# A recommendation model's count matmuls, split into two halves of the partitions

## The chip, the cores and the metric

The kernel runs on one core of a Trainium2 chip. The metric is device time in microseconds (us) from the start to the end of the program. The engines are called PE (TensorE, matmuls), DVE (VectorE), ACT (ScalarE), POOL (GpSimd) and SP (SyncE, which only issues DMAs here). They run side by side and wait for each other through semaphores.

## The reference

A model of the kind used for recommendations. There are 2048 samples, 26 tables of 12500 rows of 64 numbers, and for each sample and table 20 indices, whose rows are summed ("pooled").

```python
x = _mlp(dense_x, bot, sigmoid_last=False)                  # 13 -> 512 -> 256 -> 64
pooled = jax.vmap(lambda tab, ix: jnp.take(tab, ix, axis=0).sum(axis=1))(tables, indices)
Tcat = jnp.concatenate([x[:, None, :], jnp.transpose(pooled, (1, 0, 2))], axis=1)
Z = jnp.einsum('bim,bjm->bij', Tcat, Tcat)
li, lj = jnp.tril_indices(ni, k=-1)
R = jnp.concatenate([x, Z[:, li, lj]], axis=1)
return _mlp(R, top, sigmoid_last=True)                      # 415 -> 512 -> 256 -> 1
```

## The kernel before, in words

Of the 26 tables, 5 are gathered by indirect DMAs on POOL. For the other 21 (`TP`) the pooling is a matmul: a matrix of counts (how often a sample uses a table row) times the table. The table lies in SBUF as 128 partitions of 98 rows (`SPAN`), so row r is at partition r // 98 and position r % 98. A position is split again: 33 columns (`COLS`) by 3 fields. A count's field is coded as a weight of 1, 2^8 or 2^16, so that one int32 holds the three counts of a column, and its bytes are read as fp8 later.

A table is worked off in 4 blocks of 512 samples (`NB`). Six samples (`GS`) with 20 indices each make a group: 120 indices (`GK`), one on each of 120 partitions. A block has 86 groups. For a group, DVE makes two operands from the indices: `onehot_p` [120 x 128], one where the index is in that partition, and `onehot_c` [120 x 198], which has for each of 33 columns and 6 samples the weight of the field, or nothing. `onehot_c` is the product of `weighted_c` (made once a block, L980 and L982) and `sample_mask`, which keeps of the six samples the one the index belongs to. One matmul of the two (L647, "count matmul") gives the counts of six samples in PSUM. Four groups (`UG`) make a unit, with two PSUM banks; units use two such pairs of banks by turns (`unit_ps`). ACT copies a unit from PSUM into `counts` as int32 (L788, `unpack_unit`). A block has 22 units, the last with two groups. DVE makes the one-hots for two units at a time (`onehot_pair`, L994 for rows, L998 for columns), and they are held for two such pairs.

When a block's counts are there, PE adds up the table: 98 matmuls (L664, "sum matmul") of 128 rows, 128 stationary columns (64 numbers in a high and in a low fp16 part) and 512 moving columns, the counts of 512 samples.

The order on PE is written by hand in `phase(t, k, tn, kn)`: for each unit u, first the count matmuls of unit u of the next block, then four sum matmuls of this block; ten more sums follow at the end. Four phases make a table, and the loop runs over 20 tables. So PE alternates all the time between four count matmuls and four sum matmuls. Before a unit, PE waits for the pair's one-hots (`onehots_ready`) and for ACT's copy of the unit that had the banks before (`counts_ready`).

Beside this DVE also computes for the next table the maxima (`max_chunk`, L928), the places of the indices (L881 to L914), the low parts (L956), the pooled results (`pool_bags`) and the sums of the gathered tables (L1032). ACT makes high and low parts (L760, L767) in two of the four blocks, and converts the indices to float (`convert_indices`, L773 and L774). SP loads tables and indices.

Ahead of the loop stands the bottom MLP (L614), between whose matmuls the first block's units are counted. Its first layer has 13 rows, the other two 128. Behind the loop stand the products of the samples (L728, "gram matmuls": fp32, on 64 rows, batches of eight in partitions 0 to 63 and in 64 to 127 by turns) and the top MLP.

Of the kernel before, what the change touches and what calls it, by code (L numbers as in the profile page):

```python
# [26 lines left out]
F32 = mybir.dt.float32  # L27
F16 = mybir.dt.float16
BF16 = mybir.dt.bfloat16
I32 = mybir.dt.int32  # L30
# [17 lines left out]
def build(nc, dense_x, indices, tables, w_bot, b_bot, w_top, b_top, out):  # L48
# [9 lines left out]
    GS = P // L  # L58
    GK = GS * L
    GC = GS * COLS  # L60
# [14 lines left out]
    assert 2 * GC <= BANK and L < 32 and GROUPS <= P and 2 * D == P and SLOTS <= QUAD  # L75
# [27 lines left out]
    with ctx:  # L103
# [74 lines left out]
        sample_mask = sb(ctx, "sample_mask", [P, GS, LG], BF16)  # L178
# [5 lines left out]
        idx_raw = sb(ctx, "idx_raw", [GROUPS, BLOCKS, GK], I32)  # L184
# [20 lines left out]
        iota_s = sb(early, "iota_s", [P, GS, LG], BF16)  # L205
# [9 lines left out]
        onehot_p = sb(loop, "onehot_p", [GK, 2, 2 * SUBS, P, LG], BF16)  # L215
        onehot_c = sb(loop, "onehot_c", [GK, 2, 2 * SUBS, COLS, GS, LG], BF16)
        weighted_c = sb(loop, "weighted_c", [GK, UNITS * SUBS, COLS, LG], BF16)
        NI = BLOCKS * GROUPS
        idx_t = sb(loop, "idx_t", [GK, NI], F32)
        scratch = sb(loop, "scratch", [GK, NI], F32)  # L220
        NIP = NI + UNITS * UG - GROUPS
        place_next = sb(loop, "place_next", [GK, 3, NIP], BF16)
        place = sb(loop, "place", [GK, 3, NIP], BF16)
# [43 lines left out]
        unit_ps = [ps[:, 2 * i:2 * i + 2, :].rearrange("p b (h c) -> p (b h) c", h=2) for i in range(2)]  # L267
# [136 lines left out]
        def _(sp):  # L404
# [39 lines left out]
            sp.wait_ge(const_step, 3)  # L444
# [101 lines left out]
        def _(pool):  # L546
            def await_alone(semaphore, value):
# [5 lines left out]
            nc.gpsimd.iota(iota_p[:, :], pattern=[[0, 1]], base=0, channel_multiplier=1,  # L553
                           allow_small_or_imprecise_dtypes=True).then_inc(const_step, 1)
            nc.gpsimd.memset(idx_f, float(ABSENT)).then_inc(const_step, 1)
            pool.wait_ge(const_step, 3)
# [4 lines left out]
            nc.gpsimd.iota(iota_s[:, :, :], pattern=[[1, GS], [0, LG]], base=0, channel_multiplier=0,  # L561
# [8 lines left out]
            pool.wait_ge(const_step, 8)  # L570
            nc.gpsimd.tensor_scalar(sample_base[:, :], iota_p[:, :], ROUND, -ROUND,
                                    ALU.add, ALU.add).then_inc(const_step, 1)
            pool.wait_ge(const_step, 9)
# [33 lines left out]
        def _(pe):  # L607
# [10 lines left out]
            def turn_indices(t, first=False):  # L618
                pe.wait_ge(idx_converted, 2 * t + 2)
                if not first:  # L620
                    pe.wait_ge(idx_copied, t)
                for k in range(BLOCKS):
                    last = nc.tensor.transpose(idx_ps[0:GK, k * GROUPS:(k + 1) * GROUPS], idx_f[:, k, :],
                                               ident[0:GROUPS, 0:GROUPS])
                last.then_inc(idx_turned, 1)
# [10 lines left out]
            def count_unit(t, k, u, first=False):  # L636

                n = UNITS * (BLOCKS * t + k) + u
                if u % 2 == 0:
                    pe.wait_ge(onehots_ready, PAIRS * (BLOCKS * t + k) + u // 2 + 1)  # L640
                if not (first and u < 2):
                    pe.wait_ge(counts_ready, n - 1)
                r = (PAIRS * k + u // 2) % 2
                for g in units_of(u):
                    x = g % UG
                    sub, lane = u % 2 * SUBS + x // LG, x % LG
                    last = nc.tensor.matmul(unit_ps[u % 2][:, x, 0:GC], onehot_p[:, r, sub, :, lane],  # L647
                                            onehot_c[:, r, sub, :, :, lane].rearrange("p c s -> p (c s)"),
                                            start=True, stop=True)
                last.then_inc(unit_counted, 1)  # L650
# [95 lines left out]
        def _(act):  # L746
# [23 lines left out]
            def convert_indices(t):  # L770

                act.wait_ge(idx_loaded, 32 * t + 32)
# [9 lines left out]
            def unpack_unit(t, k, u):  # L782

                n = UNITS * (BLOCKS * t + k) + u
                act.wait_ge(unit_counted, n + 1)
# [90 lines left out]
        def _(dve):  # L876
            def copy_indices(t, first=False):
                dve.wait_ge(idx_turned, t + 1)
                if not first:
                    dve.wait_ge(idx_ready, t)  # L880
                nc.vector.tensor_copy(idx_t[:, :], idx_ps[0:GK, 0:NI]).then_inc(idx_copied, 1)  # L881
# [86 lines left out]
            def weight_columns(t, k, first=False):  # L968

                n = BLOCKS * t + k  # L970
                if not first:
                    dve.wait_ge(onehots_ready, PAIRS * n)
                whole = [GK, UNITS * SUBS, COLS, LG]
# [5 lines left out]
                iota = iota_by_unit[0:GK, 0:COLS, :].rearrange("p (a c) g -> p a c g", a=1).to_broadcast(whole)  # L979
                tt(weighted_c[:, :, :, :], iota, by_unit(1), ALU.is_equal).then_inc(weighted, 1)  # L980
                dve.wait_ge(weighted, 2 * n + 1)
                tt(weighted_c[:, :, :, :], weighted_c[:, :, :, :], by_unit(2), ALU.mult).then_inc(weighted, 1)  # L982
                dve.wait_ge(weighted, 2 * n + 2)

            def onehot_pair(t, k, d, first=False):

                if not (first and d < 2):
                    dve.wait_ge(unit_counted, UNITS * (BLOCKS * t + k) + 2 * d - 2)
                r = (PAIRS * k + d) % 2
                whole = [GK, 2 * SUBS, P, LG]  # L990
                g0 = k * GROUPS + 2 * UG * d
                at = place[:, 0, g0:g0 + 2 * UG].rearrange("p (u a g) -> p u a g", a=1, g=LG).to_broadcast(whole)
                iota = iota_by_unit[0:GK, :, :].rearrange("p (a c) g -> p a c g", a=1).to_broadcast(whole)
# [3 lines left out]
                mask = sample_mask[0:GK, :, :].rearrange("p (a s) g -> p a s g", a=1).to_broadcast(whole)  # L997
# [177 lines left out]
```

## Time and profile before

| | |
|---|---|
| median of 3 runs | 3101.85 us (3100.75 to 3103.76) |
| the profiled execution | 3101.67 us, its span 3099.8 us |
| PE / DVE / ACT / POOL busy | 96% / 83% / 60% / 66% |
| count matmuls, sum matmuls | 7224 and 8232 |
| mean granted clock of TensorE | 0.956 of full |

An engine's busy share is the union of its instructions' times. Matmuls are pipelined: the duration shown for one is longer than what it costs in a row of them, so costs are best read from starts. The profile names for each idle time what ended it.

### The profile page before, as it was taken

How to read it: one execution, taken by the hardware profiler on the slowest of the kernel's cores; microseconds unless marked ns; L12 is line 12 of the kernel's file. 1: busy time of each engine (PE TensorE's matmuls, PEld its weight loads, DVE VectorE, ACT ScalarE, POOL GpSimd, SP SyncE). 2: the span in 40 equal slices, each digit the busy share in tenths (PEclk: the TensorE clock that was granted, in tenths of full speed). 3: DMA queues.
4: the chain of work that ended last, by engine and by line, in shares of the span. 5: the costliest groups of instructions: out<-in, count | busy, mean ns of one | idle time of the engine just before them, and what ended most of it. 6: DMA issues, size and time to landing. Idle time of an engine off the chain costs nothing.

```text
span 3099.8 us, 50958 instructions
## 1 busy us (share of the span) xinstructions
PE 2968.0 (96%) x16980; PEld 1728.8 (56%) x16980; DVE 2566.2 (83%) x3442; ACT 1864.5 (60%) x2391; POOL 2051.5 (66%) x1639
## 2 busy tenths in 40 slices
PE   6999999999999999999999999999999999999999
PEld 2455555555555555555555555555555555569774
DVE  4599999999999999999999999999999999833221
ACT  3566757667576676666766757667576676622222
POOL 3278878787787887888888888888888888000000
PEclk8899999999999999999999999999999999985668
DMA  2112122122121221212212112122121221064411
GB/s 65 60 27 69 35 62 71 25 72 67 29 69 25 71 67 30 69 26 70 71 25 69 50 46 71 24 71 67 29 69 27 69 69 24 25 97 81 75 28 28
DMA packets 165642, 164.47 MB, mean 53 GB/s; under 512 B 108859, under 2 KB 127083, under 8 KB 160231
## 3 DMA queue, kind: packets, MB, share of 16 engines
q1 hardware_dynamic: 114135, 110.94, 13.0%
q0 software_dynamic: 51200, 52.53, 8.6%
q10 hardware_dynamic: 272, 0.52, 0.1%
q8 instruction: 23, 0.38, 0.1%
q14 instruction: 12, 0.10, 0.0%
HBM read 143.83 MB, written 20.05 MB: 53 GB/s over the span
## 4 chain that ended last, share of the span: by engine, by line
PE 57%; DVE 33%; issue 7%; ACT 2%; DVEq 1%; DMA 0%; SPq 0%; POOL 0%; ACTq 0%; POOLq 0%
PE ps L664 31%; PE ps L647 13%; DVE onehot_c L998 11%; PE ps L728 7%; PE ps L614 5%; DVE rowmax L928 4%; DVE onehot_p L994 4%; DVE weighted_c L982 3%; DVE weighted_c L980 3%; DVE pooled_sb L1006 2%; DVE pooled_sb L1009 1%; DVE rows L1032 1%; DVE bags_out L1032 1%; ACT counts L788 1%; ACT parts L767 0%
## 5 line engine op out<-in xcount | busy, mean ns | idle before, releaser
L588 POOL DMA_INDIRECT rows<-in_L_rec_tables,look x1600 | 2034.6, 1272 | 547.2 <-issue 484.0
L664 PE MATMUL ps<-counts,parts 128*128 128x512 fp8e3 x8232 | 2158.0, 388 | 0.0
L788 ACT CAST counts<-ps 128x792 int32<-128x792 f32 (+1 forms) x1848 | 1511.5, 824 | 886.2 <-PE ps L647 877.2
L664 PEld LDWEIGHTS ps<-counts,parts 128*128 128x128 f16 x8232 | 778.9, 96 | 596.6 <-issue 0.8
L647 PE MATMUL ps<-onehot_c,onehot_p 120*128 120x198 bf16 x7224 | 956.9, 252 | 90.4 <-DVE onehot_c L998 79.8
L647 PEld LDWEIGHTS ps<-onehot_c,onehot_p 120*128 120x128 bf16 x7224 | 659.6, 98 | 624.1 <-ACT counts L788 137.5
L998 DVE TENSOR_TENSOR onehot_c<-weighted_c,sample_mask 120x1584 bf16<-120x1584 bf16 x924 | 902.7, 977 | 0.0
L994 DVE TENSOR_TENSOR onehot_p<-iota_by_unit,place 120x1024 bf16<-120x1024 bf16 x924 | 634.9, 687 | 211.9 <-PE ps L647 186.2
L376 DVE COPY zt<-ps 32x208 f32<-32x208 f32 x128 | 87.5, 683 | 189.2 <-PE ps L728 188.3
L728 PE MATMUL ps<-slots 64*128 64x104 f32 x1024 | 220.3, 464 | 2.9 <-DMA slots<-pooled 2.9
L728 PEld LDWEIGHTS ps<-slots 64*128 64x128 f32 x1024 | 219.6, 365 | 4.9 <-DVE w_top1T L398 3.1
L1032 DVE TENSOR_REDUCE rows<-rows 128x64 f32<-128x384 f32 (+1 forms) x240 | 189.2, 788 | 0.0
L376 ACT COPY zt<-ps 32x208 f32<-32x208 f32 x128 | 63.4, 496 | 190.1 <-PE ps L728 189.4
L956 DVE SCALAR_TENSOR_TENSOR raw<-raw,coef_next,parts 128x896 f32<-128x896 f32 x147 | 168.7, 1148 | 3.2 <-ACT parts L760 1.8
L928 DVE TENSOR_REDUCE rowmax<-raw 128x1 f32<-128x896 f32 x147 | 155.8, 1074 | 0.0
L760 ACT ACTIVATE parts<-raw,coef_next 128x896 f16<-128x896 f32 x147 | 152.6, 1038 | 0.0
L980 DVE TENSOR_TENSOR weighted_c<-iota_by_unit,place 120x2904 bf16<-120x2904 bf16 x84 | 140.2, 1669 | 3.9
L982 DVE TENSOR_TENSOR weighted_c<-weighted_c,place 120x2904 bf16<-120x2904 bf16 x84 | 140.4, 1671 | 2.9
L767 ACT ACTIVATE parts<-raw 128x896 f16<-128x896 f32 x147 | 139.4, 948 | 0.0
L1006 DVE TENSOR_SCALAR pooled_sb<-ps,coef 64x512 f32<-64x512 f32 x84 | 63.5, 756 | 29.7 <-PE ps L664 27.0
L603 POOL MEMSET slots<- 128x1280 f32 x2 | 2.3, 1164 | 100.7 <-PE ps L664 100.7
L614 PE MATMUL ps<-feats,w_top0T 128*128 128x512 f32 (+1 forms) x128 | 67.4, 667 | 0.0
(82 smaller groups left out, 559.6 us busy)
## 6 DMA issues: line engine op xcount, KB each, us to landing
raw<-in_L_rec_tables SPq DMA_DIRECT2D x21, 1792.0 KB
raw<-in_L_rec_tables SPq DMA_DIRECT2D x21, 1344.0 KB
rows<-in_L_rec_tables,look POOLq DMA_INDIRECT x1600, 2.8
pooled<-pooled_sb SPq DMA_DIRECT2D x84, 128.0 KB, 2.3
slots<-pooled SPq DMA_DIRECT2D x30, 352.0 KB, 7.9
products<-zt SPq DMA_DIRECT2D x16, 351.0 KB
idx_raw<-in_r_indices SPq DMA_DIRECT2D x21, 159.4 KB
gathered<-bags_t SPq DMA_DIRECT2D x42, 64.0 KB
```

What stands on the lines that cost most here:

```text
L588: nc.gpsimd.indirect_dma_start(rows[:, s, l, :], None, rows_flat, bass.IndirectOffsetOnAxis(ap=look[:, c, s * PL + l:s * PL + l + 1].bitca ...
L614: last = nc.tensor.matmul(into[i % len(into)][0:mm, :], w, x, start=(k == 0), stop=(k == len(terms) - 1))
L647: last = nc.tensor.matmul(unit_ps[u % 2][:, x, 0:GC], onehot_p[:, r, sub, :, lane], onehot_c[:, r, sub, :, :, lane].rearrange("p c s -> p ...
L664: mm = nc.tensor.matmul(acc[k % 2][:, 0:NB], parts[:, j, :], count_bytes[k % 2][:, j % COLS, 0:NB, j // COLS], start=(j == 0), stop=(j == ...
L728: last = nc.tensor.matmul(banks[2 * (b % 3) + x // 4][:, x % 4 * P:x % 4 * P + GW], tile[:, g, :, :].rearrange("p k s -> p (k s)"), tile[: ...
L788: nc.scalar.copy(counts[k % 2][:, :, u * UG * GS:(u * UG + g) * GS].rearrange("p c (g s) -> p g c s", s=GS), unit_ps[u % 2][:, 0:g, 0:GC]. ...
L928: nc.vector.tensor_reduce(rowmax[:, q:q + 1], raw[:, q * CJ:(q + 1) * CJ, :], AX.XY, ALU.max, apply_absolute_value=True).then_inc(rowmax_p ...
L980: tt(weighted_c[:, :, :, :], iota, by_unit(1), ALU.is_equal).then_inc(weighted, 1)
L982: tt(weighted_c[:, :, :, :], weighted_c[:, :, :, :], by_unit(2), ALU.mult).then_inc(weighted, 1)
L994: tt(onehot_p[:, r, :, :, :], iota, at, ALU.is_equal)
L998: tt(onehot_c[:, r, :, :, :, :].rearrange("p u c s g -> p (u c) s g"), cols, mask, ALU.mult).then_inc(onehots_ready, 1)
L1032: nc.vector.tensor_reduce(dst, src, AX.X, ALU.add).then_inc(piece_free, 1)
```

## The change

A group keeps six samples, but they are laid out as two times three: the 60 indices of three samples on partitions 0 to 59 and the 60 of the other three on partitions 64 to 123. Each count matmul becomes two, one for each half, on 60 rows, with 99 moving columns (33 columns by 3 samples) in place of 198. The two halves write to different PSUM banks. So `onehot_c` and `sample_mask` have half the columns, on 128 partitions; `onehot_p` keeps its 128. ACT's copy reads both banks and puts the samples in the old order, so that `counts` and all that follows are as before. The indices are loaded in two DMAs instead of one (apart from the last group's), converted in three copies instead of two, and turned over 128 columns instead of 120. POOL makes the partition numbers for each half by a separate iota.

```diff
-    GS = P // L
+    HALVES = 2
+    HS = P // HALVES // L
+    HK = HS * L
+    HP = P // HALVES
+    HC = HS * COLS
+    GS = HALVES * HS
     GK = GS * L
-    GC = GS * COLS
...
-        unit_ps = [ps[:, 2 * i:2 * i + 2, :].rearrange("p b (h c) -> p (b h) c", h=2) for i in range(2)]
+        unit_ps = [ps[:, 2 * i:2 * i + 2, 0:UG * HC] for i in range(2)]
...
-                sp.dma_start(idx_raw[0:GROUPS - 1, :, :],
-                             flat[:, 0:cut].rearrange("k (g r) -> g k r", r=GK)).then_inc(idx_loaded, 16)
+                for h in range(HALVES):
+                    sp.dma_start(idx_raw[0:GROUPS - 1, :, h * HP:h * HP + HK],
+                                 flat[:, 0:cut].rearrange("k (g h r) -> h g k r", h=HALVES, r=HK)[h]
+                                 ).then_inc(idx_loaded, 16)
...
+            for h in range(HALVES):
+                pool.wait_ge(const_step, h + 1)
+                nc.gpsimd.iota(iota_p[h * HP:(h + 1) * HP, :], pattern=[[0, 1]], base=0, channel_multiplier=1,
+                               allow_small_or_imprecise_dtypes=True).then_inc(const_step, 1)
...
-                    last = nc.tensor.matmul(unit_ps[u % 2][:, x, 0:GC], onehot_p[:, r, sub, :, lane],
-                                            onehot_c[:, r, sub, :, :, lane].rearrange("p c s -> p (c s)"),
-                                            start=True, stop=True)
-                last.then_inc(unit_counted, 1)
+                    for h in range(HALVES):
+                        rows_h = slice(h * HP, h * HP + HK)
+                        last = nc.tensor.matmul(unit_ps[u % 2][:, h, x * HC:(x + 1) * HC],
+                                                onehot_p[rows_h, r, sub, :, lane],
+                                                onehot_c[rows_h, r, sub, :, :, lane].rearrange("p c s -> p (c s)"),
+                                                start=True, stop=True)
+                        if g == units_of(u)[-1]:
+                            last.then_inc(unit_counted, 1)
...
-                nc.scalar.copy(idx_f[0:GROUPS - 1, :, TAIL * L:], idx_raw[0:GROUPS - 1, :, TAIL * L:]
-                               ).then_inc(idx_converted, 1)
+                for cols in (slice(TAIL * L, HK), slice(HP, HP + HK)):
+                    nc.scalar.copy(idx_f[0:GROUPS - 1, :, cols], idx_raw[0:GROUPS - 1, :, cols]
+                                   ).then_inc(idx_converted, 1)
...
-                    counts[k % 2][:, :, u * UG * GS:(u * UG + g) * GS].rearrange("p c (g s) -> p g c s", s=GS),
-                    unit_ps[u % 2][:, 0:g, 0:GC].rearrange("p g (c s) -> p g c s", s=GS),
+                    counts[k % 2][:, :, u * UG * GS:(u * UG + g) * GS].rearrange(
+                        "p c (g h s) -> p h g c s", h=HALVES, s=HS),
+                    unit_ps[u % 2][:, :, 0:g * HC].rearrange("p h (g c s) -> p h g c s", c=COLS, s=HS),
                 ).then_inc(counts_ready, 1)
...
-                whole = [GK, 2 * SUBS * COLS, GS, LG]
+                whole = [P, 2 * SUBS * COLS, HS, LG]
```

On PE, at the head of the table loop, the order before was the following; `ps` is PSUM, the names behind the arrow are the operands, and the sizes those of the output.

```order
L647 MATMUL ps<-onehot_c,onehot_p 128x198 x4
L664 MATMUL ps<-counts,parts 128x512 x4
L640 REGISTER_ALU
L642 REGISTER_ALU
L647 MATMUL ps<-onehot_c,onehot_p 128x198 x4
L664 MATMUL ps<-counts,parts 128x512 x4
```

The same place on PE in the changed kernel, whose line numbers are higher by 9 to 15:

```order
L658 MATMUL ps<-onehot_c,onehot_p 128x99 x8
L677 MATMUL ps<-counts,parts 128x512 x4
L649 REGISTER_ALU
L651 REGISTER_ALU
L658 MATMUL ps<-onehot_c,onehot_p 128x99 x8
L677 MATMUL ps<-counts,parts 128x512 x4
```

Nothing moved; each unit has eight count matmuls of 99 columns where it had four of 198, in the same place between the sums.

On DVE, in the first block of the loop's body, a pair of units before:

```order
L994 TENSOR_TENSOR onehot_p<-iota_by_unit,place 120x1024
L998 TENSOR_TENSOR onehot_c<-weighted_c,sample_mask 120x1584
L955 REGISTER_ALU
L956 SCALAR_TENSOR_TENSOR raw<-raw,coef_next,parts 128x896
L1025 REGISTER_ALU
```

and in the changed kernel:

```order
L1009 TENSOR_TENSOR onehot_p<-iota_by_unit,place 128x1024
L1013 TENSOR_TENSOR onehot_c<-weighted_c,sample_mask 128x792
L970 REGISTER_ALU
L971 SCALAR_TENSOR_TENSOR raw<-raw,coef_next,parts 128x896
L1040 REGISTER_ALU
```

The row one-hots keep their size, the column one-hots have half of it.

## Rows read from the trace of the kernel before

**Rows 1.** The page: span; busy time of PE; the clock granted, in 40 slices.
```profile
span 3099.8 us, 50958 instructions
...
PE 2968.0 (96%) x16980; PEld 1728.8 (56%) x16980; DVE 2566.2 (83%) x3442; ACT 1864.5 (60%) x2391; POOL 2051.5 (66%) x1639
...
PEclk8899999999999999999999999999999999985668
```

**Rows 2.** The page: the chain that ended last, shares of the span by engine.
```profile
PE 57%; DVE 33%; issue 7%; ACT 2%; DVEq 1%; DMA 0%; SPq 0%; POOL 0%; ACTq 0%; POOLq 0%
```

**Rows 3.** Groups by form: line, engine, names, shapes, count | busy us, mean ns | idle.
```profile
L664 PE MATMUL ps<-counts,parts 128*128 128x512 fp8e3 x8232 | 2158.0, 388 | 0.0
L788 ACT CAST counts<-ps 128x792 int32<-128x792 f32 x1764 | 1471.7, 839 | 870.7 <-PE ps L647 861.8 <-DMA pooled<-x_bot 4.1
L647 PE MATMUL ps<-onehot_c,onehot_p 120*128 120x198 bf16 x7224 | 956.9, 252 | 90.4 <-DVE onehot_c L998 79.8 <-ACT counts L788 8.4
L998 DVE TENSOR_TENSOR onehot_c<-weighted_c,sample_mask 120x1584 bf16<-120x1584 bf16 x924 | 902.7, 977 | 0.0
...
L994 DVE TENSOR_TENSOR onehot_p<-iota_by_unit,place 120x1024 bf16<-120x1024 bf16 x924 | 634.9, 687 | 211.9 <-PE ps L647 186.2 <-DVE pooled_sb L1009 13.8 <-DVE coef L963 0.2
...
L774 ACT CAST idx_raw<-idx_raw 85x320 f32<-85x320 int32 x21 | 9.7, 462 | 0.0
```

**Rows 4.** A table's four blocks: length, PE, PEld, DVE, ACT, POOL busy, clock, DMA.
```profile
1382.30:1414.60 32.30, 30.94 (x194) 17.69 (x192) 29.33 (x39) 22.72 (x30) 26.51 (x20) 1.00 0.38 128
1414.60:1447.90 33.30, 30.75 (x186) 16.71 (x184) 32.64 (x44) 18.14 (x22) 26.60 (x23) 1.00 0.15 31
1447.90:1478.50 30.60, 30.16 (x187) 17.18 (x185) 27.39 (x43) 18.17 (x22) 24.22 (x23) 1.00 0.14 27
1478.50:1508.80 30.30, 30.30 (x187) 17.07 (x185) 28.57 (x34) 24.84 (x31) 24.91 (x18) 1.00 0.12 24
```

**Rows 5.** Timeline of PE in a steady stretch: start us, us, instruction, count.
```profile
1500.42 1.06 PE L664 MATMUL ps<-counts,parts 128*128 128x512 fp8e3 x4
1501.32 0.53 PE L647 MATMUL ps<-onehot_c,onehot_p 120*128 120x198 bf16 x4
1501.70 1.07 PE L664 MATMUL ps<-counts,parts 128*128 128x512 fp8e3 x4
```

**Rows 6.** The chain in order of time: ends of two blocks of the last table.
```profile
2705.31 3.16 PE ps L664 x14
...
2735.29 25.27 PE ps L664 x112
```

**Rows 7.** Who waited for whom: us in total, times, longest us.
```profile
PE ps L647 <- DVE onehot_c L998: 79.8, 100, 1.5
...
PE ps L647 <- ACT counts L788: 8.4, 21, 1.9
```

**Rows 8.** Timeline of PE in the bottom MLP, 128-row and 13-row neighbours.
```profile
66.24 0.53 PE L647 MATMUL ps<-onehot_c,onehot_p 120*128 120x198 bf16 x4
66.61 3.62 PE L614 MATMUL ps<-h_bot,w_bot1T 128*128 128x512 f32 x8
...
74.39 0.53 PE L647 MATMUL ps<-onehot_c,onehot_p 120*128 120x198 bf16 x4
74.85 1.12 PE L614 MATMUL ps<-xT,w_bot0T 13*128 13x512 f32 x2
```

**Rows 9.** Timeline from 74.385 to 74.42 us: weight loads behind a 13-row matmul.
```profile
74.38 0.12 PEld L647 LDWEIGHTS ps<-onehot_c,onehot_p 120*128 120x128 bf16 x2 [0.76 <-issue]
```

**Rows 10.** Timeline of PE, gram matmuls: windows 2828.69:2829.2 and 2829.70:2830.50.
```profile
2828.42 1.14 PE L728 MATMUL ps<-slots 64*128 64x104 f32 x6
...
2829.38 1.53 PE L728 MATMUL ps<-slots 64*128 64x104 f32 x5
```

**Rows 11.** Timeline of PE in the second block of a table, with an idle time.
```profile
1439.71 0.54 PE L647 MATMUL ps<-onehot_c,onehot_p 120*128 120x198 bf16 x4 [1.46 <-DVE onehot_c L998]
```

**Rows 12.** The chain at the start: SP's issue of the first index load.
```profile
8.52 0.37 SPq L414
```

More of the change, by code:

```diff
@@ L74, in build @@
     assert B % NB == 0 and UNITS % 2 == 0 and BLOCKS % 2 == 0 and SPAN % CHUNKS == 0
-    assert 2 * GC <= BANK and L < 32 and GROUPS <= P and 2 * D == P and SLOTS <= QUAD
+    assert UG * HC <= BANK and L < 32 and GROUPS <= P and 2 * D == P and SLOTS <= QUAD
     assert TP * ROWS + ABSENT <= T * ROWS
@@ L204, in build @@
         iota_p = sb(early, "iota_p", [P, 1], F32)
-        iota_s = sb(early, "iota_s", [P, GS, LG], BF16)
+        iota_s = sb(early, "iota_s", [P, HS, LG], BF16)
         early.close()
@@ L214, in build @@
         parts = sb(loop, "parts", [P, SPAN, 2 * D], F16)
-        onehot_p = sb(loop, "onehot_p", [GK, 2, 2 * SUBS, P, LG], BF16)
-        onehot_c = sb(loop, "onehot_c", [GK, 2, 2 * SUBS, COLS, GS, LG], BF16)
-        weighted_c = sb(loop, "weighted_c", [GK, UNITS * SUBS, COLS, LG], BF16)
+        onehot_p = sb(loop, "onehot_p", [P, 2, 2 * SUBS, P, LG], BF16)
+        onehot_c = sb(loop, "onehot_c", [P, 2, 2 * SUBS, COLS, HS, LG], BF16)
+        weighted_c = sb(loop, "weighted_c", [P, UNITS * SUBS, COLS, LG], BF16)
         NI = BLOCKS * GROUPS
-        idx_t = sb(loop, "idx_t", [GK, NI], F32)
-        scratch = sb(loop, "scratch", [GK, NI], F32)
+        idx_t = sb(loop, "idx_t", [P, NI], F32)
+        scratch = sb(loop, "scratch", [P, NI], F32)
         NIP = NI + UNITS * UG - GROUPS
-        place_next = sb(loop, "place_next", [GK, 3, NIP], BF16)
-        place = sb(loop, "place", [GK, 3, NIP], BF16)
+        place_next = sb(loop, "place_next", [P, 3, NIP], BF16)
+        place = sb(loop, "place", [P, 3, NIP], BF16)
         look = sb(loop, "look", [P, GB, L], I32)
@@ L443, in _ @@
             sp.sem_inc(pooled_free, 1)
-            sp.wait_ge(const_step, 3)
+            sp.wait_ge(const_step, 4)
             load_indices(0)
@@ L560, in _ @@
                            allow_small_or_imprecise_dtypes=True).then_inc(const_step, 1)
-            nc.gpsimd.iota(iota_s[:, :, :], pattern=[[1, GS], [0, LG]], base=0, channel_multiplier=0,
+            nc.gpsimd.iota(iota_s[:, :, :], pattern=[[1, HS], [0, LG]], base=0, channel_multiplier=0,
                            allow_small_or_imprecise_dtypes=True).then_inc(const_step, 1)
@@ L622, in turn_indices @@
                 for k in range(BLOCKS):
-                    last = nc.tensor.transpose(idx_ps[0:GK, k * GROUPS:(k + 1) * GROUPS], idx_f[:, k, :],
+                    last = nc.tensor.transpose(idx_ps[:, k * GROUPS:(k + 1) * GROUPS], idx_f[:, k, :],
                                                ident[0:GROUPS, 0:GROUPS])
@@ L972, in weight_columns @@
                     dve.wait_ge(onehots_ready, PAIRS * n)
-                whole = [GK, UNITS * SUBS, COLS, LG]
+                whole = [P, UNITS * SUBS, COLS, LG]
                 def by_unit(i):
@@ L977, in by_unit @@
                         "p (u a g) -> p u a g", a=1, g=LG).to_broadcast(whole)
-                iota = iota_by_unit[0:GK, 0:COLS, :].rearrange("p (a c) g -> p a c g", a=1).to_broadcast(whole)
+                iota = iota_by_unit[:, 0:COLS, :].rearrange("p (a c) g -> p a c g", a=1).to_broadcast(whole)
                 tt(weighted_c[:, :, :, :], iota, by_unit(1), ALU.is_equal).then_inc(weighted, 1)
@@ L987, in onehot_pair @@
                 if not (first and d < 2):
-                    dve.wait_ge(unit_counted, UNITS * (BLOCKS * t + k) + 2 * d - 2)
+                    dve.wait_ge(unit_counted, HALVES * (UNITS * (BLOCKS * t + k) + 2 * d - 2))
                 r = (PAIRS * k + d) % 2
-                whole = [GK, 2 * SUBS, P, LG]
+                whole = [P, 2 * SUBS, P, LG]
                 g0 = k * GROUPS + 2 * UG * d
                 at = place[:, 0, g0:g0 + 2 * UG].rearrange("p (u a g) -> p u a g", a=1, g=LG).to_broadcast(whole)
-                iota = iota_by_unit[0:GK, :, :].rearrange("p (a c) g -> p a c g", a=1).to_broadcast(whole)
+                iota = iota_by_unit[:, :, :].rearrange("p (a c) g -> p a c g", a=1).to_broadcast(whole)
                 tt(onehot_p[:, r, :, :, :], iota, at, ALU.is_equal)
-                whole = [GK, 2 * SUBS * COLS, GS, LG]
+                whole = [P, 2 * SUBS * COLS, HS, LG]
                 cols = weighted_c[:, 2 * SUBS * d:2 * SUBS * (d + 1), :, :].rearrange("p u (c a) g -> p (u c) a g", a=1).to_broadcast(whole)
-                mask = sample_mask[0:GK, :, :].rearrange("p (a s) g -> p a s g", a=1).to_broadcast(whole)
+                mask = sample_mask[:, :, :].rearrange("p (a s) g -> p a s g", a=1).to_broadcast(whole)
                 tt(onehot_c[:, r, :, :, :, :].rearrange("p u c s g -> p (u c) s g"), cols, mask,
```

21 lines of the change are left out of this document (10 added, 11 removed).

## The prediction

> **What bounds the kernel now.** I read the page first. TensorE is busy 96% of the span and its clock is granted in full, the 2.4 GHz level, from slice 3 on until the late stages [rows 1]; but the chain that ended last runs only 57% over PE and 33% over DVE [rows 2]. So two engines share the bound, and the question is where each of them sets the pace. The windows of the four blocks of one table show it [rows 4]: 32.3, 33.3, 30.6 and 30.3 us, 126.5 together. In the second block DVE is busy 32.64 of 33.30 us; in the other three it has slack and PE has none. The blocks of the last table, where DVE has no next table to prepare, follow each other at 2735.29 - 2705.31 = 29.98 us [rows 6]. That is PE's own pace: in steady state four sum matmuls take 1501.32 - 1500.42 = 0.90 us and four count matmuls 1501.70 - 1501.32 = 0.38 us [rows 5], 0.37 in another place [rows 8]. So one sum matmul costs 0.225 us and one count matmul 0.0915 us of PE's time, though the "mean of one" in [rows 3] reads 388 and 252 ns, since matmuls overlap. Check: 98 x 0.2255 + 86 x 0.0915 = 29.97 us. At the 2.4 GHz level 512 columns are 213 ns and 198 columns are 82.5 ns, so each matmul pays about 9 to 12 ns beyond its columns.
>
> What is above 29.98 us in a block is waiting: 6.6 us per table in [rows 4]. Over the whole program PE waits 79.8 us in 100 places for the column one-hots of DVE, and 8.4 us in 21 for ACT [rows 7]. The profile counts a wait only from the modelled end of the last matmul, 0.16 us after its 0.225 us slot (388 - 225 ns), so DVE holds PE up by about 79.8 + 100 x 0.16 = 96 us. [Rows 11] is the longest of a table, 1.46 us counted, 1.6 us real.
>
> **The change, part by part.** It has a gain on DVE, a gain and a cost on PE, and small change elsewhere.
>
> DVE: the column one-hots shrink from 1584 to 792 elements. Row one-hots of 1024 elements take 687 ns and column one-hots of 1584 take 977 ns [rows 3]: 0.52 ns an element, so 792 elements are about 567 ns. Saved: 924 x 0.41 = 379 us of DVE, 4.5 us a block. The block at 32.64 us busy falls to 28.1 and none is near PE's pace. DVE works two pairs of units, some 5 us, ahead; at the head of a block (two weighting passes, a pooling, pairs) three pairs less 0.41 us each give 1.2 us back there. I take the 96 us as gone; at worst a fifth of it stays.
>
> PE, columns: each count matmul of 198 columns on 120 rows becomes two of 99 columns on 60 rows, at partitions 0 and 64. If both halves of the array run at once, a pair needs 99 columns, 41 ns, plus overhead. That they can is shown by the gram matmuls, which also use 64 rows, in one half or the other by turns: where only one half's are at work, five starts lie in 1.12 us (2829.38 to the window's end at 2830.50), about 0.27 us apart; where one half's batch overlaps the other's, six starts lie in 0.78 us (2828.42 to 2829.20) [rows 10]. With both halves at work the rate about doubles, weight loads included. A pair then costs between 41 + 10 = 51 ns (the overhead paid once, in parallel) and 41 + 20 = 61 ns (each of the two weight loads holds up both). I take the middle, 56 ns, since no row has two halves in 16-bit types. Over the 83 blocks that run beside sums: 83 x 86 = 7138 pairs, 7138 x (91.5 - 56) ns = -253 us; with the ends -289 and -218.
>
> PE, switching: PE now goes from matmuls on 128 rows to matmuls on 60 rows and back in every unit. The trace of before has such switches in the bottom MLP. There the four count matmuls of a unit take 66.61 - 66.24 = 0.37 us when the matmuls around them have 128 rows, and 74.85 - 74.39 = 0.46 us when they have 13 [rows 8]. The 0.46 holds one switch away and one weight load after a switch that nothing hides (the two loads that fit into 0.12 us in [rows 9], so about 0.01 us). So one switch with its load costs 0.09 to 0.10 us. Two a unit, 22 units a block, 83 blocks: 1826 x 2 x 0.10 = +365 us, at the low end 1826 x 2 x 0.09 = +329. This is a cost that no other engine's work can hide, because PE is the engine that ends last in each of these units.
>
> The Trainium skill, "TensorEngine Tiling (Array Packing)", section "Key Properties", says that changing the tiling mode drains TensorE, and that tiles load weights and multiply in parallel. By that rule, the trace agrees on both: [rows 8] and [rows 10].
>
> ACT: the count copy still has 792 elements, 839 ns [rows 3], read from two runs of 396 instead of four of 198, and written in runs of 3 instead of 6. I see no reason for another time; it is hidden, as ACT is busy 18 to 25 us of a block [rows 4]. At +0.1 us a copy it would still be hidden. The index conversion is one copy more, about 0.2 us a table (462 ns for 320 elements [rows 3] are split), hidden except where ACT is late already: 0 to +4 us.
>
> SP and Pool: one more index load per table, 0.37 us on SP [rows 12]; in the loop it lies beside 30 us of nothing to do, at the start it delays the weight loads by that much. With one more iota the start costs +0.5 to +1 us. In the bottom MLP 22 units gain some 0.03 us each and half of them gain a switch: nought.
>
> Sum: -253 + 365 = +112 on PE, -96 for the waits, +1 at the start, +2 for ACT: **+19 us**. The profiled execution took 3101.67 us (span 3099.8), 0.2 us from the median, so I forecast 3121 us, 0.6% slower. The mechanism in a sentence: DVE's relief and the halved columns are real, and two drains a unit eat both.
>
> **The rivals.**
> A. The pair is as cheap as its columns and the switch at its low end: -289 + 329 - 96 + 1 = -55 us, 3047 us; if the other waiting in [rows 4] went too (6.6 x 20 - 96 = 36 us), down to 3011. For it: [rows 10] shows a clean doubling. Against it: the 9 to 12 ns beyond the columns look like the weight load, and there are twice as many.
> Beside A stands the Trainium skill, "TensorE: Matmul & The Clock Gate", section "Measured speedup vs the span model": a further tile adds only about 4 ns to the span. By that, an estimate, a pair would be 45 ns and the time 3042 us; no row here has 16-bit halves to show it.
> The sign turns where pair time and switch add up: 7138 x p + 3652 x s must fall by 19 us, for instance p = 53 ns at s = 0.10.
> B. The halves do not overlap in this order (one half's load waits for the other's matmul): a pair costs 2 x 51 = 102 ns, +75 instead of -253: 3449 us. For it: in [rows 10] whole batches overlap, not neighbours in the queue; against it: the batches' loads ran in parallel too.
> C. DVE's waits stay, because they come from order and not from load (pooling waits for the block's last sum): 3121 + 96 = 3217 us. Against it: the windows of [rows 4] say load, and [rows 6] shows none without it.
> D. The change moves nothing that can be measured, gains and drains cancelling, within 6 us of 3102; in the terms above that is p near 53 ns.
>
> **How the numbers follow.** Forecast case, 3108 to 3200: 0.43. A: 0.30. B: 0.08. C, or a slower ACT copy: 0.07. D: 0.12. Likeliest time 3121 us. Below 3035 and above 3200 I leave about 0.15; the range 3035 to 3200 takes in A down to its low end and the high end of my own terms (-218 + 365 - 77 + 5 = +75, 3177). A measurement of this kernel can tell 0.2%, 6 us, from no change: faster 0.30, same 0.12, slower 0.58.
>
> **What would show it.** In a steady stretch of the timeline four sums and eight halves should take 0.90 + 0.20 + 0.22 = 1.32 us a unit in place of 1.28; the four blocks about 31.3 us each, all alike, the second no longer the longest; DVE's column one-hots near 567 ns and DVE's share near 70%; PE's waits for DVE near nought. A unit of 1.25 us would mean A, one of 1.5 us B, a second block of 33 us C. I am wrong altogether if the drain between 60 and 128 rows is not that of 13 rows, or if ACT's copy grows beyond 1.2 us and takes PE's place as the bound.

## The result: 0.8% faster, where 0.6% slower was forecast

The changed kernel takes 3076.27 us (median of 4 runs, 3074.39 to 3079.76) where the kernel before takes 3101.3; the ratio is 0.992, with a 95% interval of 0.990 to 0.994. On another chip (the kernel before at 3109.4 us there) it took 3083.87, ratio 0.992 again. The forecast was 3121 us, with 0.30 for "faster". The time lies in the stated range of 3035 to 3200 and on the other side of no change.

The page after, first the busy times and then the chain that ended last by engine; it answers to [rows 1] and [rows 2]:

```profile
span 3074.7 us, 65587 instructions
...
PE 3007.2 (98%) x24204; PEld 1328.9 (43%) x24204; DVE 2211.8 (72%) x3442; ACT 2123.2 (69%) x2412; POOL 1755.0 (57%) x1640
...
PE 85%; ACT 5%; DVE 4%; issue 4%; SPq 1%; DMA 1%; DVEq 0%; ACTq 0%; POOL 0%; POOLq 0%
```

DVE has left the chain (33% before, 4% now) and PE fills it. The four blocks of a table, as in [rows 4] with the same columns; the first line answers to 32.30, the second to 33.30, the third to 30.60, and the last is the block ahead of them, which answers to 30.30:

```profile
1371.70:1403.10 31.40, 31.40 (x281) 12.95 (x278) 24.02 (x36) 25.57 (x31) 22.34 (x21) 1.00 0.41 134
1403.10:1433.90 30.80, 30.80 (x272) 12.16 (x270) 29.10 (x46) 21.48 (x22) 21.29 (x21) 1.00 0.17 32
1433.90:1464.80 30.90, 30.90 (x275) 12.27 (x272) 23.09 (x42) 21.39 (x22) 21.04 (x21) 1.00 0.13 27
1340.00:1371.70 31.70, 31.00 (x272) 12.17 (x270) 24.96 (x36) 27.74 (x31) 22.85 (x21) 1.00 0.13 27
```

The block that DVE set at 33.30 us is now 30.80, with DVE busy 29.10 in it. The quiet block of 30.60 has gone up to 30.90, the last from 30.30 to 31.70; PE is idle in it for 0.7 us, of which more below. The sum of a table falls from 126.5 to 124.8 us.

The steady stretch of PE, to be held against [rows 5]:

```profile
1405.68 1.07 PE L677 MATMUL ps<-counts,parts 128*128 128x512 fp8e3 x4
1406.69 0.36 PE L658 MATMUL ps<-onehot_c,onehot_p 60*128 60x99 bf16 x8
1406.98 1.07 PE L677 MATMUL ps<-counts,parts 128*128 128x512 fp8e3 x4
1407.99 0.37 PE L658 MATMUL ps<-onehot_c,onehot_p 60*128 60x99 bf16 x8
```

Four sums now stand 1.01 us long where they stood 0.90, for a switch lies at their end: in the trace's records the first half starts 0.318 us behind the last sum, where two sums stand 0.225 apart. The eight halves take 0.29 to 0.30 us in place of 0.37 to 0.38, with the other switch among it: the next sum starts 0.136 us behind the last pair. The two matmuls of a pair start 3 ns apart. A unit is 1.30 us long, 0.03 more than before.

The whole in three pieces, from the starts of the first sum matmul of each block: the stretch up to the first block went from 115.2 to 117.6 us, the 83 blocks to the last from 2623.1 to 2594.0, and what follows from 361.6 to 363.2. Together -25 us. The first and the last piece are no firm numbers: the changed kernel run again on another chip reached its first block after 115.9 us. The blocks again in two: PE's own pace rose from 29.98 to 30.84 us a block, 83 x 0.86 = +71 us; what stands above that pace fell from 2623.1 - 83 x 29.98 = 135 to 2594.0 - 83 x 30.84 = 34 us, -101.

Not all of the 34 us is waiting for another engine. In each table PE also transposes the indices and the pooled rows of the gathered tables; from start to start that takes 0.50 us a table before and 0.69 after, 10 and 14 us in all. And the changed kernel stands still once a table where PE's loop jumps back:

```profile
1371.41 0.36 PE L658 MATMUL ps<-onehot_c,onehot_p 60*128 60x99 bf16 x8 [0.48 <-DVE onehot_c L1013]
...
L709 PEldq COMPARE_BRANCH  x20: 83/3368/3665, 241.6 to 2615.6; - x20
...
L696 PEldq COMPARE_BRANCH  x20: 76/208/239, 239.6 to 2643.6; - x20
```

The second line is the branch at the end of PE's loop in the changed kernel (shortest, median and longest in ns), the third the same branch before: 3.4 us in place of 0.21. Five register instructions, 0.5 us, stand between it and the next count matmul. The 14 sums that are queued ahead of it last 3.3 us, so PE runs dry. From the last sum to the next count matmul pass 0.83 to 1.20 us in the 19 turns that jump back, and 0.32, as at every other switch, in the last, which does not. Together the turns cost 12 us (18 us in the run on the other chip); before, they cost nothing. The profile puts this idle time down to DVE, but PE needs only the first pair of one-hots there, and that was ready 2 us earlier. Why the branch takes longer no run shows; the loop's body has 1080 count and sum matmuls on PE where it had 736. That leaves about 124 us of waiting for other engines before and 8 after, -116.

### The profile page after: what moved, and what is told of

It is laid out like the page before. It is cut to its first block, busy times and chain, and to the rows that moved or that the text cites. A ratio compares the mean times of both kernels' runs of the same rounds, so it can differ in the third digit from the quotient of the medians.

```text
span 3074.7 us, 65587 instructions
## 1 busy us (share of the span) xinstructions
PE 3007.2 (98%) x24204; PEld 1328.9 (43%) x24204; DVE 2211.8 (72%) x3442; ACT 2123.2 (69%) x2412; POOL 1755.0 (57%) x1640
## 4 chain that ended last, share of the span: by engine, by line
PE 85%; ACT 5%; DVE 4%; issue 4%; SPq 1%; DMA 1%; DVEq 0%; ACTq 0%; POOL 0%; POOLq 0%
PE ps L677 57%; PE ps L658 16%; PE ps L741 7%; PE ps L623 5%; ACT counts L802 3%; ACT parts L780 1%; DVE weighted_c L997 1%; DVE weighted_c L995 1%; DVE onehot_c L1013 1%; ACT parts L773 1%; DVE onehot_p L1009 0%; DVE bags_out L1047 0%; SPq L495 0%; ACT h_bot L815 0%; DMA look_in<-in_r_indices 0%
## 5 line engine op out<-in xcount | busy, mean ns | idle before, releaser
L802 ACT CAST counts<-ps 128x792 int32<-128x792 f32 (+1 forms) x1848 | 1775.9, 980 | 600.7 <-PE ps L658 591.6
L597 POOL DMA_INDIRECT rows<-in_L_rec_tables,look x1600 | 1732.7, 1083 | 799.8 <-issue 476.8
L1009 DVE TENSOR_TENSOR onehot_p<-iota_by_unit,place 128x1024 bf16<-128x1024 bf16 x924 | 638.9, 691 | 512.0 <-PE ps L658 475.8
L677 PEld LDWEIGHTS ps<-counts,parts 128*128 128x128 f16 x8232 | 645.9, 96 | 752.3 <-issue 1.1
L658 PEld LDWEIGHTS ps<-onehot_c,onehot_p 60*128 60x128 bf16 x14448 | 381.8, 95 | 838.2 <-issue 767.0
L658 PE MATMUL ps<-onehot_c,onehot_p 60*128 60x99 bf16 x14448 | 665.6, 209 | 20.3 <-DVE onehot_c L1013 12.5
L1013 DVE TENSOR_TENSOR onehot_c<-weighted_c,sample_mask 128x792 bf16<-128x792 bf16 x924 | 521.7, 565 | 0.0
L995 DVE TENSOR_TENSOR weighted_c<-iota_by_unit,place 128x2904 bf16<-128x2904 bf16 x84 | 140.1, 1668 | 3.9
L997 DVE TENSOR_TENSOR weighted_c<-weighted_c,place 128x2904 bf16<-128x2904 bf16 x84 | 140.3, 1671 | 2.9
```

Source lines behind the costliest of these rows:

```text
L597: nc.gpsimd.indirect_dma_start(rows[:, s, l, :], None, rows_flat, bass.IndirectOffsetOnAxis(ap=look[:, c, s * PL + l:s * PL + l + 1].bitca ...
L658: last = nc.tensor.matmul(unit_ps[u % 2][:, h, x * HC:(x + 1) * HC], onehot_p[rows_h, r, sub, :, lane], onehot_c[rows_h, r, sub, :, :, lan ...
L677: mm = nc.tensor.matmul(acc[k % 2][:, 0:NB], parts[:, j, :], count_bytes[k % 2][:, j % COLS, 0:NB, j // COLS], start=(j == 0), stop=(j == ...
L802: nc.scalar.copy(counts[k % 2][:, :, u * UG * GS:(u * UG + g) * GS].rearrange("p c (g h s) -> p h g c s", h=HALVES, s=HS), unit_ps[u % 2][ ...
L1013: tt(onehot_c[:, r, :, :, :, :].rearrange("p u c s g -> p (u c) s g"), cols, mask, ALU.mult).then_inc(onehots_ready, 1)
```

## The experiments

### DVE's relief alone

The kernel before, in which the column one-hots are those of three samples, and PE reads each twice. The outputs are not the model's, since half of the samples' counts are left out.

```diff
-        onehot_c = sb(loop, "onehot_c", [GK, 2, 2 * SUBS, COLS, GS, LG], BF16)
+        onehot_c = sb(loop, "onehot_c", [GK, 2, 2 * SUBS, COLS, HS, LG], BF16)
...
-                                            onehot_c[:, r, sub, :, :, lane].rearrange("p c s -> p (c s)"),
+                                            onehot_c[:, r, sub, :, :, lane].rearrange("p (a c) s -> p a (c s)", a=1
+                                                ).to_broadcast([GK, 2, HS * COLS]),
```

> The kernel before with DVE's relief alone: onehot_c has half the columns (the mask of three samples), and the count matmul still streams 198 columns by reading the 99 twice, so the counts are those of three samples twice over. Theory (two effects of opposite sign): PE stays at 29.98 us a block, DVE's waits of 96 us go: about 3005 us, clearly faster than the changed kernel's 3076. Rival (the gain came from PE's pairs, relief does little, because DVE's waits come from the order of its work): 3080 to 3100 us.

3000.32 us, ratio 0.963 (0.958 to 0.968): all of the theory's gain and more than the change's. Three of the four blocks of a table, with the block that DVE had bound in third place:

```profile
1301.90:1332.20 30.30, 30.30 (x186) 17.36 (x185) 24.31 (x36) 24.86 (x31) 22.66 (x20) 1.00 0.13 24
1332.20:1362.90 30.70, 30.70 (x192) 18.03 (x191) 24.59 (x37) 22.74 (x30) 23.97 (x22) 1.00 0.43 137
1362.90:1393.10 30.20, 30.20 (x187) 17.48 (x186) 28.71 (x46) 18.17 (x22) 22.32 (x21) 1.00 0.17 32
```

With half of the column one-hots, 33.30 us become 30.20. PE's work is as before but for the moving operand read twice, which makes PE's own pace 30.17 us a block in place of 29.98. PE's idle time for DVE's one-hots falls from 79.8 to 1.2 us. So the waits were DVE's load and not the order of its work; rival C of the prediction is out. What the change gains on balance, it gains here.

### PE's change alone

The changed kernel, with DVE's instruction for the column one-hots as long as before. One form of it leaves three unused samples between those that PE reads:

```diff
-                                                onehot_c[rows_h, r, sub, :, :, lane].rearrange("p c s -> p (c s)"),
+                                                onehot_c[rows_h, r, sub, :, 0:HS, lane],
```

> The changed kernel with DVE's old load: onehot_c is made with six samples' columns again (1584 elements, the last three unused), PE reads three of them. Theory: PE's own block is 30.84 us in place of 29.98, +71 us, and the DVE waits stay but for what the slower PE absorbs (up to 0.86 us a block): 3120 to 3172 us, slower than before. Rival (PE's halves are the gain): not above 3100 us.

3350.95 us, ratio 1.075 (1.070 to 1.081), far above both theories. The cause stands in the timeline of PE:

```profile
1505.50 1.07 PE L677 MATMUL ps<-counts,parts 128*128 128x512 fp8e3 x4
1506.51 0.52 PE L658 MATMUL ps<-onehot_c,onehot_p 60*128 60x99 bf16 x8
1506.96 1.08 PE L677 MATMUL ps<-counts,parts 128*128 128x512 fp8e3 x4
```

The eight halves take 0.45 us in place of 0.29; between the starts of two pairs lie 84 to 88 ns in place of about 48. On PE the moving operand is different: 99 columns in 33 runs of three, with a gap after each. (The output is written as 33 by 3 too, but to the same places.) The run tells nothing about DVE; the next one leaves PE's operands as they are, and its eight halves take 0.29 us again. DVE writes a tile twice as large, of which every second part is read; the values in it are not the right ones.

```diff
-        onehot_c = sb(loop, "onehot_c", [P, 2, 2 * SUBS, COLS, HS, LG], BF16)
+        onehot_c2 = sb(loop, "onehot_c", [P, 2, 2 * SUBS, 2, COLS, HS, LG], BF16)
...
-                whole = [P, 2 * SUBS * COLS, HS, LG]
+                whole = [P, 2 * 2 * SUBS * COLS, HS, LG]
```

> The changed kernel with DVE's old load, PE's operands untouched: the column one-hots are 1584 elements an instruction as before, in a tile twice as large, of which PE reads every second unit's part (the values are not the right ones). In the run before, the stepped moving operand alone cost PE 84 instead of 51 ns a pair, which this leaves out. Theory (PE +71 us, DVE's relief worth 100 us): DVE sets the second block again at 33.4 us, the others stand at 30.9 to 32.5: 3130 to 3172 us, slower than the kernel before. Rival (PE's halves are the gain): at or below 3100 us.

3134.12 us, ratio 1.006 (1.004 to 1.008). The block that DVE binds, with DVE's own instruction:

```profile
1430.80:1463.90 33.10, 31.07 (x274) 12.17 (x272) 32.42 (x44) 21.46 (x22) 26.70 (x22) 1.00 0.16 31
...
L1014 DVE TENSOR_TENSOR onehot_c<-weighted_c,sample_mask 128x1584 bf16<-128x1584 bf16 x924 | 902.6, 977 | 0.0
```

DVE is busy 32.42 of 33.10 us again, though PE's matmuls are those of the change. So without DVE's relief the change makes the kernel slower by 0.6% (the longer branch and ACT's longer copy included), and the relief alone makes it faster by 3.7%; together they give 0.8%. They do not add up, since the slower PE hides a part of DVE's lateness when DVE is late: the quiet block is 30.59 us long before and 31.23 here, the block that DVE binds 33.4 and 33.1.

### What a switch costs: two units between switches

The changed kernel, with the count matmuls of two units behind each other and then eight sums. The result is the same and half of the switches are gone.

```diff
-                for u in range(UNITS):
+                for u in range(0, UNITS, 2):
...
-                    j1 = SPAN if u == UNITS - 1 else PER_UNIT * (u + 1)
+                    j1 = SPAN if u == UNITS - 2 else PER_UNIT * (u + 2)
                     await_rows(t, k, PER_UNIT * u, j1)
                     count_unit(tn, kn, u)
-                    for j in range(PER_UNIT * u, PER_UNIT * (u + 1)):
+                    count_unit(tn, kn, u + 1)
+                    for j in range(PER_UNIT * u, PER_UNIT * (u + 2)):
```

> The changed kernel with two units counted one behind the other, then eight sums: half of the switches between 60 and 128 rows. Theory (a switch with its weight load costs 0.10 us, nothing hides it): 11 round trips of 0.20 us fewer a block, 83 blocks: -183 us, near 2893 us, if ACT keeps up. Rival (ACT's copies of 1.0 us come in twos and its waits take the place): 2950 to 3020 us, with PE waiting for ACT counts in the blocks where ACT makes the parts. If drains cost nothing, 3076 or more.

2972.18 us, ratio 0.954 (0.949 to 0.959). The timeline of PE in a quiet block:

```profile
1353.33 1.98 PE L677 MATMUL ps<-counts,parts 128*128 128x512 fp8e3 x8
1355.23 0.56 PE L658 MATMUL ps<-onehot_c,onehot_p 60*128 60x99 bf16 x16
1355.73 1.98 PE L677 MATMUL ps<-counts,parts 128*128 128x512 fp8e3 x8
```

Sixteen halves take 0.49 to 0.50 us where eight take 0.29 to 0.30 (from first start to the first sum's start, 492 and 297 ns in the middle of all stretches). The difference is four pairs without a switch: 195 / 4 = 49 ns a pair. The quiet blocks fall from 30.84 to 28.55 us, 2.29 us for 11 round trips: 0.208 us a round trip, 0.104 a switch. The drain is real, and it is priced as forecast. The two blocks in which ACT also makes the parts of the next table are 31.3 and 31.5 us long, so the whole falls within the rival's 2950 to 3020 and not near 2893: PE's wait for ACT is visible in the stretch of such a block,

```profile
1332.49 0.36 PE L658 MATMUL ps<-onehot_c,onehot_p 60*128 60x99 bf16 x8
1333.15 0.36 PE L658 MATMUL ps<-onehot_c,onehot_p 60*128 60x99 bf16 x8 [0.30 <-ACT counts L803]
```

The same edit in the kernel before, which has no switch in its loop (the diff is the same):

> The kernel before with two units counted one behind the other, then eight sums; there is no switch between row modes in it. Theory (the 141 us of the same edit in the changed kernel are switches): the quiet blocks stay at 29.98 us, with ACT's waits the whole is 3100 to 3150 us. Rival (the longer runs of sums help PE by themselves, in weight loads or otherwise): 2960 to 3050 us.

3139.82 us, ratio 1.007 (1.005 to 1.010). In its timeline eight counts take 0.73 us, twice 0.365, and eight sums 1.80, twice 0.90:

```profile
1484.05 0.89 PE L647 MATMUL ps<-onehot_c,onehot_p 120*128 120x198 bf16 x8
1484.78 1.97 PE L664 MATMUL ps<-counts,parts 128*128 128x512 fp8e3 x8
1486.58 0.89 PE L647 MATMUL ps<-onehot_c,onehot_p 120*128 120x198 bf16 x8
```

The quiet block is 30.55 us long, where it was 30.59. So longer stretches are worth nothing in themselves. What they bring in the changed kernel are the switches, and 10 of the 12 us of the loop's turn: 18 sums, 4.2 us, are queued ahead of the branch there.

### Do the halves run at once?

Both matmuls of a pair on partitions 0 to 59, so that the upper three samples get wrong counts:

```diff
-                        rows_h = slice(h * HP, h * HP + HK)
+                        rows_h = slice(0, HK)
```

> The changed kernel with both matmuls of a pair on partitions 0 to 59 (the upper samples' counts are wrong). Theory (a pair costs 51 ns because two halves of the array run at once): a pair costs 102 ns here, 7138 x 51 ns = +364 us, 3440 us. If the 51 ns were the floor of issuing two small matmuls, nothing changes: 3076 us.

3396.1 us (one run), where 3440 was the theory's and 3076 the rival's.

```profile
1501.52 0.55 PE L658 MATMUL ps<-onehot_c,onehot_p 60*128 60x99 bf16 x8
1502.00 1.07 PE L677 MATMUL ps<-counts,parts 128*128 128x512 fp8e3 x4
```

The eight now take 0.48 us. Less the 0.10 of the switch that is 0.38, 47 ns for one matmul and 95 for a pair, where the pair in two halves takes 49. The halves overlap almost wholly; the rival of an issue floor is out.

The halves in another order, the four of the lower half and then the four of the upper:

```diff
-                for g in units_of(u):
+                for h in range(HALVES):
...
-                    for h in range(HALVES):
+                    for g in units_of(u):
```

> The changed kernel with a unit's four matmuls of the lower half first and the four of the upper half behind them. If the halves overlap only as neighbours in the queue, a unit takes 7 x 51 + 200 ns in place of 4 x 51 + 200 for its counts, +0.15 us a unit: 3076 + 280 = 3350 us. If PE lets the upper half's matmuls overtake the waiting ones of the lower half, as whole batches of gram matmuls did, it stays within 20 us of 3076.

3094.72 us (one run), nowhere near 3350. It ran on another chip than the change; its quiet blocks are 31.06 us long, where the change's are 30.84, which is 18 us in 83 blocks.

```profile
1421.06 0.37 PE L658 MATMUL ps<-onehot_c,onehot_p 60*128 60x99 bf16 x8
1421.37 1.07 PE L677 MATMUL ps<-counts,parts 128*128 128x512 fp8e3 x4
```

Eight halves take 0.31 us, 0.01 to 0.02 more than in pairs. Their starts still come in twos, 13 to 14 ns apart. If the upper half's four waited for their turn, the first of them could start no earlier than the lower half's last: six steps of 47 ns and the 0.136 us to the next sum, 0.42 us. So PE starts the upper half's matmuls while the lower half's, which stand ahead of them in the program, still wait. That the halves alternate in the program is of little weight.

### ACT's copy

The prediction saw no reason for a longer copy. It went from 839 to 998 ns. The kernel before, with its copy in runs of three and an outer loop of two, and the same result:

```diff
-                    counts[k % 2][:, :, u * UG * GS:(u * UG + g) * GS].rearrange("p c (g s) -> p g c s", s=GS),
-                    unit_ps[u % 2][:, 0:g, 0:GC].rearrange("p g (c s) -> p g c s", s=GS),
+                    counts[k % 2][:, :, u * UG * GS:(u * UG + g) * GS].rearrange("p c (g h s) -> p h g c s", h=2, s=GS // 2),
+                    unit_ps[u % 2][:, 0:g, 0:GC].rearrange("p g (c h s) -> p h g c s", h=2, s=GS // 2),
```

> The kernel before, with ACT's copy of a unit walking the same 792 elements in runs of three in an outer loop of two, as the changed kernel does, in both source and target. If the copy's 839 to 998 ns came from its access pattern, it takes 950 to 1000 ns here, with 10 to 30 us more in the whole. If it came from PE writing two banks at once while ACT reads, it stays at 839 ns and the time at 3101.

```profile
L788 ACT CAST counts<-ps 128x792 int32<-128x792 f32 x1764 | 1738.0, 1001 | 632.3 <-PE ps L647 623.2 <-DMA pooled<-x_bot 4.0
```

1001 ns without any of PE's change: the pattern of access makes it longer, and not PE's writing to two banks. The time is 3112.53 us, ratio 0.9996 (0.997 to 1.002), so 0.16 us more a copy costs nothing there that the medians show, where 10 to 30 us were expected. In the trace the last block of a table, in which ACT makes parts, is 31.03 us long, where it was 30.32.

What it costs the changed kernel: its copy with target runs of 12, the halves one after the other (the samples then stand in another order in the counts, so the outputs are not the reference's). Beside it, on the same chip, the changed kernel itself.

```diff
-                        "p c (g h s) -> p h g c s", h=HALVES, s=HS),
-                    unit_ps[u % 2][:, :, 0:g * HC].rearrange("p h (g c s) -> p h g c s", c=COLS, s=HS),
+                        "p c (h g s) -> p h c g s", h=HALVES, s=HS),
+                    unit_ps[u % 2][:, :, 0:g * HC].rearrange("p h (g c s) -> p h c g s", c=COLS, s=HS),
```

> The changed kernel with that copy (samples permuted in the counts). What the longer copy costs the change: if 998 ns falls to some 840, most of the 34 us that its blocks stand above PE's pace go: 3045 to 3060 us. If the waits are not ACT's, 3076.

> The changed kernel once more, on the same chip as the runs beside it: 3074 to 3080 us.

```profile
L802 ACT CAST counts<-ps 128x792 int32<-128x792 f32 x1764 | 1435.9, 820 | 863.5 <-PE ps L658 849.3 <-issue 4.8 <-DMA pooled<-x_bot 4.1
```

The copy takes 820 ns, the kernel 3074.23 us (3070.95 to 3075.69) against 3083.87 (3081.10 to 3088.12) of the changed kernel beside it, which itself lies above the 3074 to 3080 expected. The difference is 10 us, less than was expected. In the two traces the blocks stand 42 and 34 us above PE's pace. The transposes keep their 14 us and the loop's turn takes 18 and 16; what goes with the shorter copy is PE's waiting in the last block of a table, 7 us. About 3 us more lie ahead of the first block, where runs of one kernel differ by as much. So the longer copy costs the change about 7 us, and 4 us of waiting in the first block of the tables stay.

### A version faster than both

With two units between switches ACT is the next bound, and there the copy counts. The copy of that kernel walked column by column, 24 counts side by side in the target, with the right result:

```diff
-                        "p c (g h s) -> p h g c s", h=HALVES, s=HS),
-                    unit_ps[u % 2][:, :, 0:g * HC].rearrange("p h (g c s) -> p h g c s", c=COLS, s=HS),
+                        "p c (g h s) -> p c g h s", h=HALVES, s=HS),
+                    unit_ps[u % 2][:, :, 0:g * HC].rearrange("p h (g c s) -> p c g h s", c=COLS, s=HS),
```

> The kernel with two units a switch (2972 us), with ACT's copy walked column by column, so that 24 counts lie side by side in the target, with the same result. If the copy's length comes from the runs of three in its target, it falls from 975 to some 840 ns, ACT's waits in the two blocks at 31.4 us shrink, and the time is 2900 to 2950 us. If it comes from the walk over two PSUM banks or the number of loops in the source, it stays or grows: 2972 us or more.

2926.4 us (2925.21 to 2930.76), ratio to the kernel before 0.941 (0.938 to 0.944). The variant with runs of 12, in permuted order:

> The same kernel with a copy whose target runs are 12 and whose halves are walked one after the other (samples then stand in a permuted order in the counts, so the outputs are not the reference's). Between the two: about 840 ns and 2900 to 2950 us if the target's runs decide, 975 ns and 2972 us if not.

2928.85 us (one run). Both copies take 821 ns, so whether the source walks through both banks for every column does not matter; the runs in the target do. Nor is it the number of loops, which is the same in both as in the copy of 998 ns.

```profile
L803 ACT CAST counts<-ps 128x792 int32<-128x792 f32 x1764 | 1378.8, 821 | 806.5 <-PE ps L658 795.3 <-issue 6.0 <-DMA pooled<-x_bot 4.2
...
1269.30:1299.70 30.40, 29.06 (x272) 12.90 (x270) 24.86 (x36) 24.17 (x32) 24.70 (x19) 1.00 0.14 27
1299.70:1330.10 30.40, 29.65 (x283) 13.69 (x278) 24.03 (x36) 21.91 (x32) 23.63 (x23) 1.00 0.44 141
1330.10:1358.60 28.50, 28.50 (x272) 12.88 (x270) 27.86 (x44) 16.55 (x23) 22.47 (x20) 1.00 0.18 35
1358.60:1387.20 28.60, 28.60 (x277) 12.92 (x272) 24.09 (x45) 16.67 (x23) 22.63 (x22) 1.00 0.15 28
```

The two blocks that ACT holds up are 30.4 us each now, where they were 31.3 and 31.5; the two others stand at PE's pace of 28.55, which the copy doesn't touch. The batches ran on different chips, so the ratios to the kernel before are what is to be compared: 0.992 for the change, 0.954 with two units a switch, 0.941 with this copy.

## Why the prediction was wrong

The mechanism was right in its main parts: the halves run at once, the switches cost what the bottom MLP's rows said, and DVE's waits go. ACT's longer copy and the pause at the loop's turn were not in it. The sum of its terms fell 44 us too high, on the wrong side of nought.

- **The pair of halves: the step that failed.** I put it at 56 ns, the middle between 51 (columns, and the overhead once) and 61 (the overhead twice). It is 49 ns. 7138 pairs x 7.25 ns are 52 us: the term is -305 us and not -253, and that is more than the whole error. Two mistakes are in it. The lower end was built from the 9 to 12 ns that matmuls of 198 and 512 columns pay beyond their columns; the matmul of 99 columns alone in one half takes 47 ns, 6 beyond the 41 that the prediction counts for its columns. And the middle was taken "since no row has two halves in 16-bit types", though the one row that showed two halves at all showed a clean doubling, weight loads included [rows 10]. The value to take was that row's, at the low end.
- **The switch.** Forecast at 0.10 us each, measured 0.103 to 0.104 (30.84 us a block, less 98 sums of 0.2255 and 86 pairs of 0.049, leaves 4.5 us for 22 round trips): some 11 to 15 us more than forecast. PE's pace was forecast at 31.33 us a block and is 30.84: about -52 us for the pairs and +11 for the switches, together -41.
- **DVE's instruction and the waits.** The instruction was forecast at 567 ns and takes 565. The waits were forecast to fall by 96 us and fell by about 116; the 96 left out a part of the waiting that [rows 4] shows, which rival A takes in. One reading of [rows 4] was wrong: in the first block, too, PE has slack, busy 30.94 of 32.30 us. The relief alone was worth 3.7%.
- **Terms put at nothing.** The turn of PE's loop costs 12 us that no term held. "I see no reason for another time" for ACT's copy was wrong, 839 to 998 ns; it cost about 7 us, already within the waits above, where 0 to 4 were forecast for all of ACT. The page shows it as ACT's share of 69% for 60%. PE's transposes cost 4 us more.
- **The start and the end.** +1 us forecast, +4 measured (2.4 and 1.6), within what runs of one kernel differ by.

Together 71 - 116 + 12 + 4 + 4 = -25 us, the difference of the spans. Terms missed in both directions, so that the error comes out smaller than the pair's alone is partly luck. The rivals: A was the nearest, but its price of -55 us took the switch at 0.09 us, where it is 0.103; the time of 3076 us lies between A's 3047 and the 6 us around 3102 of D. The chance of 0.30 that A had was too small for a sum in which 3 ns on one unmeasured term turned the sign. The prediction said as much ("The sign turns where pair time and switch add up", at p = 53 ns), and then gave the side away on a midpoint. B is out by two runs, C by one.

The bottom MLP's rows with 13 rows were the right place to price the drain between 60 and 128 rows.

## What to carry to other kernels

A matmul on half of the rows is worth it only in long stretches: the way in and out costs about 0.1 us each, as much as two whole pairs here, so gather the matmuls of one row mode before switching. Price the parts of a change one by one: here the part that looked like a side effect, less work on DVE, carried all of the gain, and the part that gave the change its name cost 71 us until its switches were halved. When a loop's body grows, look at the turn of the loop in the trace, and check there whether the engine that the profile names for a wait had not long been done. And when a bound rests between two ends and the sum's sign hangs on it, take the end that the nearest row shows, not the middle.

## What the runs showed that was not expected

- A moving operand read in runs of three 16-bit elements with gaps between them makes PE slower: 84 to 88 ns a pair of 99 columns, against 49 for one evenly stepped run.
- PE lets matmuls of the other half overtake: four of the lower half followed by four of the upper take 0.31 us, against 0.29 to 0.30 in pairs and 0.48 all in one half.
- The branch at the end of PE's loop takes 3.4 us in the changed kernel, 0.21 before, and PE stands still behind it for some 0.6 us where 3.3 us of sums are queued ahead of it, hardly where 4.2 are. Why the branch is longer is open.
- ACT's copy of 792 elements from PSUM takes 998 to 1001 ns with target runs of three, 839 with six, 820 and 821 with 12 and 24.
- A weight load in the halves costs next to nothing while the same half's matmul runs: 47 ns for a load and 99 columns. By the difference between a sum of 512 columns and a count of 198 (225.5 and 91.5 ns, 0.43 ns a column), the columns are an estimated 42 of it.
